# Window attention after a convolution on one core: q as three fp32r products ahead of V, an earlier eviction, and work moved between engines in the first bodies and at the end

## The reference

```python
perceived = conv_depthwise_3x3(x, w_perc) + b_perc        # 128 -> 3*128 channels
hid = gelu(w_up1 @ perceived + b_up1)                     # 384 -> 256
h_new = x + w_up2 @ hid + b_up2                           # 256 -> 128
q, k, v = split(h_new @ w_qkv.T + b_qkv, 3)
scores[p] = (q * k_shifted[p]).sum(-1) / sqrt(128)        # 9 positions, zero-padded
out = h_new + sum_p softmax(scores)[p] * v_shifted[p]
```

## Time and profile before

| | us |
|---|---|
| median of three runs | 408.79 |
| lowest and highest run | 408.61, 408.90 |
| the profiled execution | 408.67 |
| its span, first to last instruction | 406.9 |
| busy in it: TensorE, VectorE, ScalarE, GpSimd | 391.0, 316.1, 305.9, 181.9 |
| mean granted TensorE clock | 0.991 |

### The profile page before, as it was taken

How to read it: one execution, slowest core, us unless ns; L and a number is a source line. 1 busy time by engine, 2 the same in 40 slices (tenths; PEclk the granted TensorE clock), 3 DMA queues, 4 the chain that set the end, 5 groups by cost and what they waited for, 6 DMA issues and landing times.

```text
span 406.9 us, 10315 instructions
## 1 busy us (share of the span) xinstructions
PE 391.0 (96%) x3650; PEld 357.5 (88%) x3650; DVE 316.1 (78%) x886; ACT 305.9 (75%) x682; POOL 181.9 (45%) x158
## 2 busy tenths in 40 slices
PE   6997998999999999999999999999999999999994
PEld 4996797898989899898989999898989989898773
DVE  5987778686868968686888868686896868785775
ACT  6643469877786878777786987778687877877782
POOL 6758753644534363544434364453436354221110
PEclk9998999999999999999999999999999999999998
DMA  7310200305040130504031040504013030301003
GB/s 259 137 64 2 92 27 4 115 1 170 2 152 19 39 130 0 168 0 168 0 101 67 8 160 0 168 0 159 9 56 112 0 103 3 105 0 53 0 29 130
DMA packets 11369, 28.58 MB, mean 70 GB/s; under 512 B 2384, under 2 KB 3024, under 8 KB 11344
## 3 DMA queue, kind: packets, MB, share of 16 engines
q1 hardware_dynamic: 10496, 28.20, 20.1%
q10 hardware_dynamic: 848, 0.05, 0.2%
HBM read 19.86 MB, written 8.39 MB: 69 GB/s over the span
## 4 chain that ended last, share of the span: by engine, by line
PE 79%; DVE 7%; ACT 3%; issue 2%; POOL 0%; DVEq 0%; ACTq 0%
PE m_ps L452 42%; PE work L462 9%; PE s_ps L524 9%; PE work L488 7%; PE work L483 7%; PE s_ps L507 5%; ACT p_sb L722 1%; ACT pt L708 1%; DVE t L826 1%; DVE y L913 1%; DVE h_around L1046 1%; DVE ps_sb L902 1%; DVE y L916 1%; DVE pt L994 0%; PE m_ps L524 0%
## 5 line engine op out<-in xcount | busy, mean ns | idle before, releaser
L452 PE MATMUL m_ps<-thi,whi 128*128 128x248 f32 (+1 forms) x576 | 170.9, 297 | 3.1 <-DVE y L926 2.5
L452 PE MATMUL m_ps<-thi,wlo 128*128 128x248 f32 (+1 forms) x576 | 161.2, 280 | 0.0
L452 PE MATMUL m_ps<-tlo,whi 128*128 128x248 f32 (+1 forms) x576 | 160.2, 278 | 0.0
L452 PEld LDWEIGHTS m_ps<-thi,whi 128*128 128x128 f32 x576 | 109.0, 189 | 10.3 <-issue 6.9
L452 PEld LDWEIGHTS m_ps<-tlo,whi 128*128 128x128 f32 x576 | 109.9, 191 | 4.2 <-issue 3.6
L452 PEld LDWEIGHTS m_ps<-thi,wlo 128*128 128x128 f32 x576 | 109.0, 189 | 0.0
L1139 POOL TENSOR_TENSOR hid_lo<-hid,hid_hi 128x1024 fp32r<-128x1024 f32 x30 | 71.9, 2398 | 20.9 <-ACT hid_hi L659 20.9
L708 ACT COPY pt<-ptc 32x256 f32<-32x256 f32 (+3 forms) x189 | 74.2, 393 | 5.0 <-DVE ptc L979 0.4
L649 ACT ACTIVATE hid<-y,b1eff 128x1024 f32<-128x1024 f32 x31 | 35.7, 1151 | 46.0 <-DVE y L926 25.6
L722 ACT ACTIVATE p_sb<-p_sb,negmax 128x101 f32<-128x101 f32 x128 | 47.0, 371 | 19.5 <-DVE negmax L960 19.5
L1116 POOL TENSOR_TENSOR fc<-xp 128x512 f32<-128x512 f32 x16 | 21.4, 1337 | 80.2 <-DVE tlo L833 78.1
(11 more groups left out here) (130 smaller groups left out, 723.6 us busy)
## 6 DMA issues: line engine op xcount, KB each, us to landing
xp<-x_planes SPq DMA_DIRECT2D x16, 640.0 KB, 5.3
xr<-x_rows SPq DMA_DIRECT2D x16, 512.0 KB, 4.1
out<-o_sb SPq DMA_DIRECT2D x28, 256.0 KB, 4.1
out<-y SPq DMA_DIRECT2D x4, 256.0 KB, 2.6
w1T<-w SPq DMA_DIRECT2D x1, 384.0 KB, 3.0
w2T<-w SPq DMA_DIRECT2D x1, 128.0 KB, 4.3
wqk_in<-w_qk SPq DMA_DIRECT2D x1, 128.0 KB, 4.3
mask_bf<-masks SPq DMA_DIRECT2D x1, 126.2 KB, 3.8
```

What stands on the lines that cost most here:

```text
L452: last = pe.matmul(m_ps[:, b, col + first:col + end], a[:, j, dy, half * P:(half + 1) * P], c[:, par, T_PLACE[j], first + by:end + by], st ...
```

## The change

The q product of every image but the last is computed from split operands: `high_h` (ScalarE) casts `h` to `h_hi`, `low_h` (VectorE) writes `h_lo = h - h_hi`, and `project_q_parts` makes six fp32r matmuls of 512 columns into `s_ps` in place of two fp32 matmuls into `work`. q stands before all of V, and both behind unit 8; the two waits for `q_done` between the parts of V move in front of the scores. `take_m13(n, 1)` stands before `high_hid(n, 0)` and all eight `exp`. In bodies 1 and 2 `sum_h` comes before `combine_y`; `low_t` of images 1 and 2 goes from GpSimd to VectorE; in body 0 GpSimd waits for `y_done` before `low_hid(0, 0)`. At the end VectorE places three rows of group 0 and ScalarE one. The weights `wqk_hi` and `wqk_lo` cost one more instruction each on ScalarE and VectorE ahead of the loop.

```diff
@@ tensor: new function, and the order of body
+            def project_q_parts(n, c):
+                if from_image(n, 2):
+                    pe.wait_ge(rmax_done, n * 8 + (4 * c - 12))
+                if from_image(n, 3):
+                    pe.wait_ge(o_done, n * 2 + (c - 5))
+                cols = slice(c * CH, (c + 1) * CH)
+                pe.wait_ge(h_hi_done, n * 2 + (c - 1))
+                pe.matmul(s_ps[:, c, :], wqk_hi[:, :], h_hi[:, cols], start=True, stop=False)
+                pe.matmul(s_ps[:, c, :], wqk_lo[:, :], h_hi[:, cols], start=False, stop=False)
+                pe.wait_ge(h_lo_done, n * 2 + (c - 1))
+                pe.matmul(s_ps[:, c, :], wqk_hi[:, :], h_lo[:, cols], start=False, stop=True).then_inc(q_ready, 1)
...
-                units(6, 7)
+                units(6, 7, 8)
                 if attn:
+                    for c in range(NCH):
+                        project_q_parts(n, c)
                     pe.wait_ge(h_done, n * 2)
-                    project_v(n, 1 - par, 0)
-                    project_q(n, 1 - par, 0, 2)
-                    project_q(n, 1 - par, 1, 0)
-                units(8)
-                if attn:
-
-                    pe.wait_ge(q_done, n * 2 - 1)
-                    project_v(n, 1 - par, 1)
-                    pe.wait_ge(q_done, n * 2)
-                    project_v(n, 1 - par, 2)
-                    scores(n, 1 - par)
+                    for part in range(3):
+                        project_v(n, 1 - par, part)
+                    for g in range(2):
+                        pe.wait_ge(q_done, n * 2 + (g - 1))
+                        score(n, 1 - par, g)
@@ scalar
+            def high_h(n, hp, c):
+
+                act.wait_ge(h_done, n * 2 + (c - 1))
+                if from_image(n, 2):
+
+                    act.wait_ge(q_ready, n * 2 - 2)
+                nc.scalar.copy(h_hi[:, c * CH:(c + 1) * CH],
+                               h_of(n - 1, hp)[:, W + c * CH:W + (c + 1) * CH]).then_inc(h_hi_done, 1)
...
-                    for row in (0, 1):
+                    for row in range(g + 1):
                         place(1, row, range(4 * g, 4 * g + 4))
...
                 if more:
                     high_t(n + 1, 1 - par)
+                if attn:
+                    for c in range(NCH):
+                        high_h(n, 1 - par, c)
                 if conv:
                     gelu(n, 0)
...
+                if conv:
+                    take_m13(n, 1)
                 if more:
                     high_hid(n, 0)
                 if attn:
                     for i in range(4):
                         exp(n, i)
-                if conv:
-                    take_m13(n, 1)
@@ vector
+            def low_h(n, hp):
+                for c in range(NCH):
+                    cols = slice(c * CH, (c + 1) * CH)
+                    dve.wait_ge(h_hi_done, n * 2 + (c - 1))
...
+                    nc.vector.tensor_tensor(h_lo[:, cols], h_of(n - 1, hp)[:, W + c * CH:W + (c + 1) * CH],
+                                            h_hi[:, cols].bitcast(F32), ALU.subtract).then_inc(h_lo_done, 1)
...
-                place(1, 2, range(0, 4))
+                place(1, 1, range(0, 4))
                 sums(n, 1)
-                place(1, 3, range(0, 4))
+                for row in (2, 3):
+                    place(1, row, range(0, 4))
                 turn_p(n, 1)
...
+                if not from_image(n, 3) and attn:
+                    sum_h(n, par)
                 if conv:
                     combine_y(n, 0)
-                if attn:
+                if from_image(n, 3) and attn:
                     sum_h(n, par)
                 if conv:
                     finish_y(n, 0)
-                if more and from_image(n, 2):
+                if attn:
+                    low_h(n, 1 - par)
+                if more:
                     low_t(n + 1, 1 - par)
@@ gpsimd
-                if more and not from_image(n, 2):
-                    for i in range(len(T_PARTS)):
-                        low_t(n + 1, 1 - par, i)
                 if conv and (not isinstance(n, int) or n + 2 < B):
                     pool.wait_ge(tlo_done, n * 2 + 4)
                     differences(n + 2, par)
                 if more:
+                    if not from_image(n, 1):
+                        pool.wait_ge(y_done, n * 2 + 2)
                     low_hid(n, 0)
```

More of the change, by code:

```diff
@@ L146, in build @@
         w2lo = sb("w2lo", [P, 2 * C], F32R)
+        h_hi = sb("h_hi", [P, PIX], F32R)
+        h_lo = sb("h_lo", [P, PIX], F32R)
+        wqk_hi = sb("wqk_hi", [P, C], F32R)
+        wqk_lo = sb("wqk_lo", [P, C], F32R)
         h_around = sb("h_around", [P, 2, W + PIX + W])
@@ L257, in build @@
         hlo_done = sem("hlo_done")
+        h_hi_done = sem("h_hi_done")
+        h_lo_done = sem("h_lo_done")
         w2hi_done = sem("w2hi_done")
+        wa_hi_done = sem("wa_hi_done")
+        wa_lo_done = sem("wa_lo_done")
         w2lo_done = sem("w2lo_done")
@@ L490, in project_v @@
                 last.then_inc(v_ready, 1)
-            def scores(n, hp):
-                for g in range(2):
-                    if from_image(n, 2):
-                        pe.wait_ge(rmax_done, n * 8 + (4 * g - 12))
-                    if from_image(n, 3) and not is_last(n):
-                        pe.wait_ge(o_done, n * 2 + (g - 5))
-                    score(n, hp, g)
             def score(n, hp, g):
@@ L569, in last_attention @@
                 for g in range(2):
-                    pe.wait_ge(pt_done, (n - 2) * PLACED + 15 + 6 * g)
-                    pe.wait_ge(pt_dve_done, 9 + 6 * g)
+                    pe.wait_ge(pt_done, (n - 2) * PLACED + 12 + 6 * g)
+                    pe.wait_ge(pt_dve_done, 12 + 6 * g)
                     values(n + 2, 1, g)
@@ L591, in body @@
                     pe.wait_ge(w2lo_done, 1)
+                    pe.wait_ge(wa_lo_done, 1)
                     pe.wait_ge(zeroed, 5)
@@ L701, in _ @@
             nc.scalar.mul(wvT[:, C:VT], wa[:, 2 * C:2 * C + 1], -SCALE).then_inc(wt_copied, 1)
+            nc.scalar.mul(wqk_hi[:, :], wa[:, C:2 * C], SCALE).then_inc(wa_hi_done, 1)
             nc.scalar.mul(bq_s[:, :], wa[:, 2 * C + 1:2 * C + 2], SCALE).then_inc(consts_done, 1)
@@ L723, in exp @@
                                      scale=-1.0, accum_out=p_sum[:, i:i + 1]).then_inc(p_done, 1)
+            def high_h(n, hp, c):
[4 more added lines that the diff above has]
+                               h_of(n - 1, hp)[:, W + c * CH:W + (c + 1) * CH]).then_inc(h_hi_done, 1)
             def take_q(n, c):
                 act.wait_ge(q_ready, n * 2 + (c - 1))
-                nc.scalar.activation(q_sb[:, c * CH:(c + 1) * CH], work[:, 2 if c == 0 else 0, :],
+                sums = work[:, 2 if c == 0 else 0, :] if is_last(n) else s_ps[:, c, :]
+                nc.scalar.activation(q_sb[:, c * CH:(c + 1) * CH], sums,
                                      ACT.Identity, bias=bq_s[:, :]).then_inc(q_done, 1)
@@ L834, in low_t @@
                                             ALU.subtract).then_inc(tlo_done, 1)
+            def low_h(n, hp):
+                for c in range(NCH):
+                    cols = slice(c * CH, (c + 1) * CH)
+                    dve.wait_ge(h_hi_done, n * 2 + (c - 1))
+                    if from_image(n, 2):
+                        dve.wait_ge(q_ready, n * 2 - 2)
+                    nc.vector.tensor_tensor(h_lo[:, cols], h_of(n - 1, hp)[:, W + c * CH:W + (c + 1) * CH],
+                                            h_hi[:, cols].bitcast(F32), ALU.subtract).then_inc(h_lo_done, 1)
             def low_weights(j, k):
@@ L888, in _ @@
             dve.wait_ge(consts_done, 2)
+            dve.wait_ge(wt_copied, 3)
+            dve.wait_ge(wa_hi_done, 1)
+            nc.vector.tensor_tensor(wqk_lo[:, :], wqk[:, :], wqk_hi[:, :].bitcast(F32), ALU.subtract).then_inc(wa_lo_done, 1)
             nc.vector.tensor_tensor(b1eff[:, :], work[:, 2, 0:2], b1[:, :], ALU.add).then_inc(b1_done, 1)
```

## The result

The changed kernel takes **401.61 us** (median of four runs, 401.60 to 401.65) against 408.83 us before (408.61 to 408.90, four runs): a ratio of 0.9825 with a 95% interval of [0.9808, 0.9842]. The prediction said 403.6 with a range from 402.3.

What follows compares the result with a forecast made beforehand. TensorE, busy 391.0 of 406.9 us, was taken to bound the steady bodies. 408.67 - 4.5 (q) - 1.2 (first bodies) - 0.2 + 0.75 (end) = 403.5, set at 403.6 us; range 402.3 to 405.6.

Steps and rivals of the forecast that it cites:

- The q product in the steady bodies: Bodies 3 to 15: six products replace 1.72 us by 1.375, saving 0.345 us a body, 4.5 us over thirteen.
- The price from `up`: Each fp32r product of q on TensorE takes 0.229 us, from twelve such products in 2.75 us.
- The slack of the chain: Steady bodies: next scores possible at S + 22.1 against TensorE's 22.88 us, so 0.8 us in hand and no new waits.
- a late `normalise`: Body 2: `normalise` on GpSimd late by 0.4 us, lengthening the binding chain from 22.1 to 22.55 us.
- The end: Body 15: 0.2 us gained by `combine` free sooner, 0.75 us lost by three more copies before the second transpose.
- The first bodies: Bodies 0 to 2: scores of body 2 at 73.7 against 74.90, a gain of 1.2 us, with the clock falling.
- first rival: Full clock in body 1: 0.7 us less, 402.9 us in all; chance 0.20.
- The last stores: From the start of the last product to the end of the span: predicted difference 0.

Runs made afterwards that it cites:

- the old end: Changed kernel with the last image's placing as before, two rows of group 0 each on ScalarE and VectorE: 400.92 us.
- the late eviction: Changed kernel with the second eviction into m13 back between the two groups of exp, behind high_hid in body 0: 402.43 us.
- The longer idle times: Changed kernel with an extra GpSimd memset in body 1 ahead of low_hid(0, 1): 401.83 us with 700 columns, 402.82 us with 1500.

## Why the prediction missed

- **The q product in the steady bodies: right.** Six products 0.23 us apart, bodies of 22.886 us (22.88 predicted), no wait for `h_lo`, 4.44 us in all. The price from `up` held. By an estimate from the 131 ns of the Trainium skill, page "TensorE: Matmul & The Clock Gate", section "Back-to-back issue gap", the stretch would have lost 12.1 us; these products, each with a weight load of its own, came 229 ns apart, and the measurement decides.
- **The slack of the chain: right in sign, off by 0.3.** The prediction had 22.1 us and 0.8 in hand; q ahead of unit 8 shows 22.4 and 0.5. That body 2 took just the 22.55 us forecast from a chain of 22.1 and a late `normalise` is thus partly luck: `p_sb` does stand in the chain there, but one of the two terms must have been smaller than written.
- **The end: right, in both terms.** +0.55 predicted for scores of body 15 to last product, +0.53 measured; the old end gives 0.75 back there and the late eviction takes 0.2.
- **The first bodies: mechanism right, size wrong. This is the step that failed**: 1.2 us predicted, 2.54 measured. Half of the miss is the sentence that "The nearest row for that is the 2.26 us of rows 9, after which the clock was at the lower level, so I take it to fall again". One row of one execution was read as a rule. The clock kept up after 1.67 us in the trace of the changed kernel, and all four of its executions took the same time. The longer idle times show that it may or may not fall after 1.9 to 2.8 us; where it fell in this place, the price was the 0.7 us worked out. The prediction carried that case as its first rival, with 0.20, though one row was all that spoke for it being the less likely. The other half is a sum of collisions that put in more turns than came: the four instructions of `combine_y` took 2.5 us and not 2.9, since two of them were stretched (to 0.90 and 0.98) and not three, and `low_hid(0, 1)` began right behind `sums_ab` (39.42) and did not wait for an instruction of `transform`. So `low_hid(0, 0)` ended at 37.67 and not 38.2, `sums_ab` at 39.4 and not 40.0, `low_hid(0, 1)` at 41.96 and not 42.75. It makes 0.7 us at the scores of body 1: 50.45 was worked out for full clock, 49.74 came.
- **The last stores: not foreseen, the second step that failed.** The sum put the stretch behind the last product at no change, without a reason, and it became 0.65 us shorter. In the profile of the kernel before there was a pause in the stream of stores; nothing of the prediction had looked at it. Why it went is not shown.
- **The first rival**, 402.9, was the nearest; with the 0.7 of the collisions it would have been 402.2, and with the stores 401.6.
- **The range.** The bound given for the first bodies, 2.5, all but holds the measured 2.54; with it the sum is 402.2, next to the lower end of 402.3. What carries the time clearly below the range is the stretch that no term stood for, the last stores.

## What to carry to other kernels

Split a result at marks that both kernels share and hold each stretch against its own term of the sum: here two of four came within 0.1 us, and the other two held the whole miss. Before forecasting a stall that depends on a state of the chip, look whether executions of the same kernel agree on it; if they don't, give it a chance and not a value. And where a new product depends on a chain through other engines, put work that is independent of it in front: here 1.04 us of it made the difference between 401.6 and 410.6 us.

## What the runs showed of the hardware

- The granted clock fell to 0.50 in some executions of a kernel and not in others. By traces, times and mean clocks: after 1.67 us of idle time in none of four, after 2.32 us at the same place in one of four, with 2.75 us not in the profiled one, but after 1.88 us elsewhere in the program in three of four. In one trace it stayed up behind 1.57 us and fell behind two waits of 0.76 and 0.73 us. What decides stays open.
- Between executions with the higher and the lower mean clock lay 0 to 0.2 us in the kernel before, where a later wait takes a fall up, 0.4 and 0.7 us in two of the others, 0.4 to 2.1 us with the memset of 1500 columns, 1.5 us with the first bodies put back (403.3 and 404.8), and 1.4 to 2.8 us with q ahead of unit 8 (410.6 and 412.0 to 413.4), where the slower ones have no trace.
- A VectorE instruction with two SBUF inputs that takes 0.41 us took 2.56 to 2.63 us beside a GpSimd subtraction of 1024 columns; beside GpSimd's memset of 1500 columns two such instructions kept their 0.41 us.
- In one trace the last 1.3 MB of stores took 0.6 us more than in another with the same work ahead of them, with one DMA issue of 1.16 us instead of 0.33.
- The cast of 512 columns that ScalarE took on and VectorE's subtraction cost nothing in the steady bodies, where TensorE never waited for them. In body 2, where twelve copies stood ahead of the cast, TensorE waited 1.0 us.
